# Local attention by probabilities times shifted inputs, with Wv Wo folded per head and the score mask copied into PSUM

## The chip, the cores and the metric

One Trainium2 chip, one of its cores. The metric is the time of one execution on the device in microseconds (us), the median of several executions; lower is better.

## The reference, cut to what matters

Input x is 4 sequences of 512 rows of 128 numbers, float32. A first attention with relative positions (16 heads of 8) comes first; the change doesn't touch it. Then come six layers. Each takes x through a local attention and a feed-forward part and adds both:

```python
half 64 columns of x are shifted down by one row (shift_tokens), then
q, k, v = x @ Wqkv                       # 16 heads of 64
q = l2norm(q) * q_scale; k = l2norm(k) * k_scale; both rotated (rotary, with scales)
sim = q k^T * 8    for windows of 32 queries, against their own 32 and the 32 keys before
sim = masked where key > query or key < query - 32, or no key there
out = softmax(sim) @ v ;  x += out @ Wo
h = layernorm(shifted x) @ W1 + b1 ;  a, gate = split(h)
x += (a * gelu(gate)) @ W2 + b2
```

`softmax(sim) @ (x Wv) @ Wo` per head equals `(softmax(sim) @ x) @ (Wv Wo)`, with x the shifted input; the changed kernel uses the right side.

## The kernel before, in words

The kernel has two parts: the first attention (to about 458 us) and `local_layers`, which holds the six layers. In the layers work is cut into tiles of 128 rows: 16 tiles per layer (4 sequences, called batches or groups, of 4 tiles), 96 tiles in all. Everything is float32. PE turns each float32 product into two records, each with its own weight load; a turn (transposition by the identity) is one.

Each engine runs a list of its own, written out by hand: a loop over rounds n (`for n in PERIODS`), in which each engine does its parts of tiles n+2 to n-4 in a fixed order, and waits on semaphores where it needs another's result. Some work comes once in four rounds, by `step = n % 4`: the feed-forward part of a whole batch (hidden products, gelu, gates, down projection) and its statistics and normalising. PSUM holds three pairs of banks (`ring`, rooms 0 to 2) and two single banks (`tpose`, `yps`). `ROOM` says which result lives in which room; `take` waits until the result that was there before has been read (`FREED`).

What is done for a tile, by engine and line of the profile:

- PE: `turn_x` (L454) turns x; `project` (L463) makes K, V and Q, two products of 512 columns each; `turn_qk` (L473) turns the rotated Q or K, eight 128x128 turns; `scores` first writes the mask as eight bf16 products (L491) and adds 64 small products of queries and keys onto it (L499, 128 records, in two halves); `turn_p` (L510) turns the probabilities; `attend` (L529) makes 64 products of V and turned probabilities (128 records, in two halves); `project_out` (L541) makes eight products with Wo. By the batch: `shift` (L551, L553), `turn_xn` (L561), `hidden` (L569, twelve records of 512 columns), `project_ffn` (L579, 24 records).
- VectorE (DVE): `rotate` (L643) multiplies Q or K with the two rotary tables, two passes over 1024 elements; `sum_squares` (L652); `take_max` (L658), `take_scores` (L666, subtracts), `sum_probs` (L674), `invert` (L681), `divide` (L687), `add_y` (L694), and by the batch `statistics` (L701, L705), `offsets`, `gate` (L721) and `add_ffn` (L730).
- ScalarE (ACT): `square` (L317), copies out of PSUM of x, Q, K, V, probabilities and the weighted sum (L328, L329, L335, L344, L355, L369, L376), `exps` (L363), and by the batch `normalise` (L393), `copy_xn` (L384) and `gelus` (L402). The gelu and the exponential each need a load of their function table.
- GpSimd (POOL): `add` (L240) adds the halves of the rotation, two additions each for Q and K; `norms` (L248 to L265) makes the inverse norms in 14 small steps; `scale` (L275) applies them to Q and to K.
- SP issues the copies: 16 per tile put V, row block by row block, where each window finds its own and the previous rows (`windows`), and the weights of the next layer (`load_layer`).

The order of PE in a round, before:

```python
project("K", n); turn_qk(0, n - 1); turn_x(n + 2)      # step 0: hidden(g - 2, 0..2)
attend(n - 3, 0)                                       # step 3: shift, step 1: project_ffn
turn_qk(1, n - 1); attend(n - 3, 1); project("V", n)
scores(n - 1, 0); project("Q", n + 1); scores(n - 1, 1)
turn_p(n - 2)                                          # step 3: turn_xn(g - 1)
project_out(n - 3)
```

## Time and profile before

| | before |
|---|---|
| three runs | 2148.3, 2149.88, 2151.88 us; median 2149.88 |
| the profiled execution | span 2143.9 us; its own time is not listed beside the runs |
| first attention | to about 458 us |
| PE busy | 2022.6 us, 94% of the span, 35763 matmuls |
| DVE, ACT, POOL busy | 1497.0 (70%), 1286.6 (60%), 1522.5 (71%) |
| mean granted TensorE clock | 0.984 |

The span runs from the first to the last instruction of one profiled execution. Busy shares are averages over stages. A timeline row gives the start, the time taken, the engine, the line, the operation, the tiles written and read, shapes and the count of merged instructions; what stands in brackets is the idle time before it and who ended it. Durations of merged rows reach from the first start to the last end, and pipelined instructions overlap a little, so what a group costs is best read from its start to the start of the next.

### The profile page before, as it was taken

What the parts mean: (1) busy time and instruction counts of PE and PEld (TensorE: products, weight loads), DVE (VectorE), ACT (ScalarE), POOL (GpSimd) and SP (SyncE); (2) the same over time, 40 slices, a digit from 0 to 9 for tenths busy, and PEclk for the clock granted to TensorE, in tenths of its full rate; (3) what the DMA queues carried; (4) which work ended last, traced back from release to release, by engine and by line L of the source; (5) the groups of instructions that cost most, each with busy time, mean ns of one, the idle gap of its engine ahead of it and who ended that gap; (6) DMA issues with size and microseconds to landing.
All of it is one profiled execution on the core that took longest, in us unless ns stands there. A gap on an engine that the chain in (4) does not pass through costs nothing.

```text
span 2143.9 us, 84229 instructions
## 1 busy us (share of the span) xinstructions
PE 2022.6 (94%) x35763; PEld 1356.1 (63%) x35763; DVE 1497.0 (70%) x2268; ACT 1286.6 (60%) x1844; POOL 1522.5 (71%) x2307
## 2 busy tenths in 40 slices
PE   4789999878999999999999999999999999999997
PEld 1455555545666667666766667666676666766675
DVE  2445454458877887777877787777877788778773
ACT  3567777634656665665656565566656666566653
POOL 3344444458878887788877778778887788777880
PEclk8899999998999999999999999999999999999998
DMA  4999999932323222242222422224222242222221
GB/s 125 289 347 355 344 357 344 348 126 61 74 62 111 68 65 65 63 113 67 72 62 62 113 62 69 65 62 120 63 66 62 63 117 70 62 62 63 68 72 43
DMA packets 120004, 261.51 MB, mean 122 GB/s; under 512 B 29092, under 2 KB 34128, under 8 KB 118864
## 3 DMA queue, kind: packets, MB, share of 16 engines
q1 hardware_dynamic: 119632, 256.13, 41.4%
q8 instruction: 285, 4.67, 1.0%
q14 instruction: 87, 0.71, 0.1%
HBM read 87.06 MB, written 68.29 MB: 72 GB/s over the span
## 4 chain that ended last, share of the span: by engine, by line
PE 68%; POOL 4%; DVE 3%; issue 2%; ACT 1%; POOLq 0%; DVEq 0%; ACTq 0%
PE ring L463 22%; PE ring L529 9%; PE ring L473 8%; PE yps L541 7%; PE ring L499 7%; PE ring L569 5%; PE ring L510 4%; PE tpose L579 3%; PE ring L491 1%; POOL roped L275 1%; DVE turned L643 1%; PE tpose L551 1%; DVE ss L652 1%; DVE stats L701 0%; POOL ss L248 0%
## 5 line engine op out<-in xcount | busy, mean ns | idle before, releaser
L643 DVE TENSOR_TENSOR turned<-ring,ropes 128x1024 f32<-128x1024 f32 x384 | 452.0, 1219 | 303.0 <-PE ring L463 303.0
L240 POOL TENSOR_TENSOR roped<-turned 128x512 f32<-128x512 f32 x384 | 522.5, 1386 | 170.4 <-PE ring L473 169.0
L463 PE MATMUL ring<-wqkv,xT 128*128 128x512 f32 x1152 | 567.4, 616 | 5.2 <-ACT xT L328 4.0
L275 POOL TENSOR_TENSOR roped<-roped,rnorm 128x1024 f32<-128x1024 f32 x192 | 361.5, 1904 | 7.5
L1170 POOL TENSOR_SCALAR less<-less,lowest 128x512 f32<-128x512 f32 x256 | 175.3, 697 | 240.0 <-DVE lowest L1139 240.0
L1139 DVE CUSTOM_DVE_ANT_0 less<-ps_b,shifted 128x512 f32<-128x512 f32 x256 | 166.6, 688 | 226.0 <-PE ps_b L1002 79.7
L463 PEld LDWEIGHTS ring<-wqkv,xT 128*128 128x128 f32 x1152 | 198.2, 192 | 161.0 <-issue 149.8
L369 ACT COPY pT<-ring 128x1024 f32<-128x1024 f32 x96 | 97.2, 1012 | 305.8 <-PE ring L510 305.8
L529 PEld LDWEIGHTS ring<-pT,vwin 64*64 64x64 f32 x12288 | 198.5, 134 | 51.9 <-issue 51.5
L317 ACT ACTIVATE squares<-ring 128x1024 f32<-128x1024 f32 x192 | 197.3, 1028 | 55.8 <-DVE turned L643 55.8
L529 PE MATMUL ring<-pT,vwin 64*64 64x32 f32 x12288 | 219.7, 220 | 4.9 <-issue 3.4
L652 DVE TENSOR_REDUCE ss<-squares 128x16 f32<-128x1024 f32 x192 | 221.3, 1184 | 1.2 <-ACT squares L317 0.9
L473 PEld LDWEIGHTS ring<-ident,roped 128*128 128x128 f32 x1536 | 174.5, 142 | 70.0 <-issue 38.4
L473 PE MATMUL ring<-ident,roped 128*128 128x128 f32 x1536 | 204.4, 276 | 8.7 <-ACT qT L335 2.9
L499 PEld LDWEIGHTS ring<-kT,qT 64*32 64x32 f32 x12288 | 139.5, 105 | 100.8 <-issue 99.2
L1002 PE MATMUL ps_b<-posm,qvT 32*128 32x512 f32 x512 | 149.1, 666 | 52.3 <-DVE lowest L1139 43.6
L541 PE MATMUL yps<-wo,oT 128*128 128x128 f32 x1536 | 188.3, 276 | 1.2 <-ACT oT L376 1.1
L541 PEld LDWEIGHTS yps<-wo,oT 128*128 128x128 f32 x1536 | 180.0, 193 | 1.6 <-ACT oT L376 1.6
L499 PE MATMUL ring<-kT,qT 64*32 64x64 f32 x12288 | 173.0, 224 | 4.9 <-issue 4.9
L1068 PEld LDWEIGHTS ps_b<-ident,less 128*128 128x128 f32 x1024 | 111.5, 142 | 94.3 <-POOL less L1170 79.2
L344 ACT COPY kT<-ring 128x1024 f32<-128x1024 f32 x96 | 97.0, 1011 | 100.6 <-PE ring L473 100.6
L1213 ACT ACTIVATE pT_a<-ps_b 128x512 f32<-128x512 f32 x256 | 141.3, 613 | 25.3 <-PE ps_b L1068 25.2
(133 smaller groups left out, 3234.7 us busy)
## 6 DMA issues: line engine op xcount, KB each, us to landing
vwin<-v SPq DMA_DIRECT2D x1536, 64.0 KB, 2.0
shifted<-scratch_w SPq DMA_DIRECT2D x64, 1024.0 KB, 12.6
scratch_w<-wrows SPq DMA_DIRECT2D x48, 1026.0 KB, 10.9
scratch_w<-x SPq DMA_DIRECT2D x16, 1026.0 KB, 10.4
wqkv<-in_l_wqkv SPq DMA_DIRECT2D x6, 1536.0 KB, 6.9
wo<-in_l_wo SPq DMA_DIRECT2D x6, 512.0 KB
w<-in_l_w SPq DMA_DIRECT2D x6, 342.0 KB
w<-in_l_w SPq DMA_DIRECT2D x6, 171.0 KB
```

Of the source, the lines that this page charges most:

```text
L240: nc.gpsimd.tensor_tensor(halves[2][:, :, side, :], halves[0][:, :, side, :], halves[1][:, :, 1 - side, :], ALU.add).then_inc(s[name + "_a ...
L275: nc.gpsimd.tensor_tensor(whole, whole, norm, ALU.mult).then_inc(s[name + "_roped"], 1)
L317: nc.scalar.activation(squares[:, n, :], ring[:, room(name.upper()), :, :].rearrange("p b c -> p (b c)"), ACT.Square).then_inc(s[name + "_ ...
L463: last = nc.tensor.matmul(out[:, half, :], xT[:, t % SEQT * P:(t % SEQT + 1) * P], wqkv[:, layer_of(t), at + half * 512:at + (half + 1) * ...
L473: last = nc.tensor.transpose(out[:, j * P:(j + 1) * P], roped[:, n, j * P:(j + 1) * P], ident[:, :])
L499: last = nc.tensor.matmul(out[W * win:W * win + W, r, j * W2:(j + 1) * W2], qT[rows, j, W * win:W * win + W], kT[rows, j, at:at + W2], sta ...
L529: last = nc.tensor.matmul(out[a * DH:(a + 1) * DH, r, at:at + W], vwin[rows, p, win, j * DH:(j + 1) * DH], pT[rows, j, W * win:W * win + W ...
L541: last = nc.tensor.matmul(out[:, 0:D], oT[:, j % 2, j // 2, :], wo[:, layer_of(t), j, :], start=j == 0, stop=j == PAIRS - 1)
L643: ins = nc.vector.tensor_tensor(turned[:, n, part, :].rearrange("p (h d) -> p h d", d=DH), heads, table, ALU.mult)
L652: nc.vector.tensor_reduce(ss[:, n * HEADS:(n + 1) * HEADS], squares[:, n, :].rearrange("p (h d) -> p h d", d=DH), AX.X, ALU.add).then_inc( ...
L1139: nc.vector.tensor_tensor_reduce(less[:, c % 2, k, :], ps[:, 2 + k, :], shifted[:, c // 2 % NR, k, c % 2, :], -SCALE0, HIGHEST, ALU.add, A ...
L1170: nc.gpsimd.tensor_scalar(less[:, c % 2, k, :], less[:, c % 2, k, :], -1.0, lowest[:, c % 2, k:k + 1], ALU.mult, ALU.add).then_inc(s["scal ...
```

## The change

V is no longer projected. Instead each head's Wv Wo (128x128) is made once per layer: Wv is turned by PE (`turn_wv`), copied by ACT, multiplied with Wo (`make_wvo`) and copied into `wvo`. Five DMA copies per tile (16 before) put the shifted input of the tile, and the same 32 rows earlier, into `xs`. The weighted sum (`attend`) is eight products of 32 rows by 512 columns: for each window of 32 rows, x of the window (stationary) times the probabilities of all 16 heads and 32 queries. The four windows lie in four row groups of PE and write to four banks. ACT copies the result in two pieces (`copy_o` OA, OB), and the output is then sixteen products (`project_out`, in two halves) instead of eight.

The probabilities are turned by VectorE in 32x32 blocks (`turn_p` there), straight into SBUF; PE's turns of them and ACT's copy go away. The mask isn't multiplied in by PE any more: ACT copies it into the scores' banks (`write_masks`), and the products add onto it. The scores' banks are now room 0, which K uses too, so the mask waits until VectorE has rotated the next tile's K.

VectorE's rotation waits for ACT's squaring (before, ACT's squaring waited for the rotation). The rotated Q and K have two buffers (`roped`). The order of all engines' lists is rewritten: Q's rotation moves to the end of VectorE's list, POOL's additions go ahead of the norms and act on tile n instead of n-1, the hidden products move from step 0 to step 1 and the down projection from step 1 to step 2. The bf16 identity and two mask fills of the tables go away. Cut to its core:

```diff
-        ROOM = {"K": 0, "QT": 1, "XT": 4, "H0": 2, "H1": 1, "H2": 0, "O": 2, "XS": 3, "F": 3, "KT": 1, "V": 0, "S": 2, "Q": 1, "PT": 0, "XN": 3, "Y": 4}
-        FREED = {"Q": ("q_squared",), "K": ("k_squared",), "V": ("v_copied",), "QT": ("qT_copied",),
-                 "KT": ("kT_copied",), "S": ("scores_taken",), "PT": ("p_copied",), "O": ("oT_copied",),
+        prev_in = [s[f"prev{n}"] for n in range(NX)]
+        OWN, PREV, LOADS = 3 * 16, 2 * 16, 10 * 16
+        CLEARED = 4
+
+
+        ROOM = {"K": 0, "QT": 1, "XT": 4, "H0": 1, "H1": 2, "H2": 0, "OA": 1, "OB": 2, "XS": 3, "F": 3, "KT": 2, "S": 0, "Q": 1,
+                "XN": 3, "Y": 4, "T": 1, "M0": 1, "M1": 2}
+        FREED = {"Q": ("q_rotated",), "K": ("k_rotated",), "QT": ("qT_copied",),
+                 "KT": ("kT_copied",), "S": ("scores_taken",), "OA": ("oa_copied",), "OB": ("ob_copied",),
                  "H": ("gelu_made", "h_ready"), "XT": ("xT_copied",), "XN": ("xnT_copied",), "XS": ("xn_made",), "Y": ("y_added",),
-                 "F": ("x_done",)}
+                 "F": ("x_done",), "T": ("wvT_copied",), "M": ("wvo_copied",)}
...
+                at_least(sp, s["o_summed"], t - NX + 1)
+                at_least(sp, prev_in[(t - NX + 1) % NX], PREV * ((t - NX + 1) // NX + 1) if t >= NX else 0)
+                sp.dma_start(xs[:, a, 0, 0:half], x[:, here, 0:half]).then_inc(s["own_in"], 16)
+                sp.dma_start(xs[1:P, a, 0, half:D], x[0:P - 1, here, half:D]).then_inc(s["own_in"], 16)
+                first = zero[P - 1:P, :] if t % SEQT == 0 else x[P - 1:P, before, half:D]
+                sp.dma_start(xs[0:1, a, 0, half:D], first).then_inc(s["own_in"], 16)
+                sp.wait_ge(s["own_in"], OWN * (t + 1))
+                sp.dma_start(xs[W:P, a, 1, :], xs[0:P - W, a, 0, :]).then_inc(prev_in[a], 16)
+                sp.dma_start(xs[0:W, a, 1, :], xs[P - W:P, b, 0, :]).then_inc(prev_in[a], 16)
...
-                    at_least(pool, s[name + "_turned"], t)
+                    at_least(pool, s[name + "_turned"], t - 1)
...
-                norms(n - 2)
-                scale(0, n - 2)
-                scale(1, n - 2)
+                add(0, n)
+                add(1, n)
+                norms(n)
+                scale(0, n)
+                scale(1, n)
+                if step == 3:
+                    deviations(g - 1)
                 if step == 1:
                     add_b2(g - 2)
-                add(0, n - 1)
-                add(1, n - 1)
-                if step == 0:
-                    deviations(g - 2)
...
-                    act.wait_ge(s[name + "_rotated"], t + 1)
+                    act.wait_ge(s[name + "_made"], t + 1)
...
+            def write_masks(t):
+
+                if live(t):
+                    n = t + 1
+                    if live(n):
+                        act.wait_ge(s["k_rotated"], n + 1)
+                    at_least(act, s["scores_taken"], t)
+                    if n % SEQT == 1 and lives(n // SEQT - 2):
+                        act.wait_ge(s["h_ready"], FCH * (n // SEQT - 1))
+                    rows = bias[:, 1 if t % SEQT == 0 else 0, :, :].unsqueeze(1).broadcast_to([P, 2, PAIRS, W2])
+                    nc.scalar.copy(ring[:, room("S"), :, :].rearrange("p r (j k) -> p r j k", k=W2), rows).then_inc(s["masked"], 1)
+
+            def copy_o(kind, t):
+
                 if live(t):
                     act.wait_ge(s["o_summed"], t + 1)
                     at_least(act, s["y_made"], t)
-                    nc.scalar.copy(oT[:, :, :, :].rearrange("p r m c -> p (r m c)"),
-                                   ring[:, room("O"), :, :].rearrange("p b c -> p (b c)")).then_inc(s["oT_copied"], 1)
+                    at = W2 if kind == "OB" else 0
+                    nc.scalar.copy(oT[:, :, at:at + W2].rearrange("c h (b q) -> c b h q", q=W),
+                                   ring[:, room(kind), :, :].rearrange("c b (h q) -> c b h q", q=W)
+                                   ).then_inc(s["oa_copied" if kind == "OA" else "ob_copied"], 1)
...
-                if step == 0:
-                    normalise(g - 2)
-                copy_p(n - 3)
-                if step == 0:
+                copy_x(n + 2)
+                square(1, n)
+                if step == 1:
                     copy_xn(g - 2)
-                square(0, n)
-                exps(n - 2)
                 copy_q(n - 1)
-                square(1, n)
-                if step == 0:
+                copy_k(n - 1)
+                copy_wv(product_layer(n, 2))
+                copy_wvo(product_layer(n, 1))
+                if step == 1:
                     gelus(g - 2, 0)
                     gelus(g - 2, 1)
                     gelus(g - 2, 2)
-                copy_k(n - 1)
-                copy_o(n - 3)
-                copy_x(n + 2)
-                copy_v(n)
+                write_masks(n - 1)
+                copy_o("OA", n - 2)
+                copy_o("OB", n - 2)
+                square(0, n + 1)
+                exps(n - 1)
+                if step == 0:
+                    normalise(g - 2)
...
+            def turn_wv(layer):
+
+                if layer is not None:
+                    pe.wait_ge(s["weights"], LOADS * (layer + 1))
+                    out = take("T", layer).rearrange("p b c -> p (b c)")
+                    for j in range(PAIRS):
+                        last = nc.tensor.transpose(out[:, j * P:(j + 1) * P], wv[:, j * P:(j + 1) * P], ident[:, :])
+                    last.then_inc(s["wv_turned"], 1)
+
+            def make_wvo(layer):
+
+                if layer is not None:
+                    pe.wait_ge(s["wvT_copied"], layer + 1)
+                    for half in range(2):
+                        out = take("M", layer, half)
+                        for j in range(half * PAIRS // 2, (half + 1) * PAIRS // 2):
                             for r in range(2):
-                                at = DH * r + W * (win % 2)
-                                first = t % SEQT == 0 and win == 0
-                                nc.tensor.matmul(out[W * win:W * win + W, r, :], identb[at:at + W, at:at + W],
-                                                 bias[at:at + W, 1 if first else 0, :, :].rearrange("p h k -> p (h k)"),
-                                                 start=True, stop=False, skip_group_check=True)
-                    for j in range(half * PAIRS // 2, (half + 1) * PAIRS // 2):
+                                rows, at = slice(r * DH, (r + 1) * DH), j % (PAIRS // 2) * D
+                                last = nc.tensor.matmul(out[:, r, at:at + D], wvT[rows, j, :], wo[rows, j, :], start=True, stop=True)
+                        last.then_inc(s["wvo_made"], 1)
...
+            def scores(t):
+                if live(t):
+                    pe.wait_ge(s["qT_copied"], t + 1)
+                    pe.wait_ge(s["kT_copied"], t + 1)
+                    pe.wait_ge(s["masked"], t + 1)
+                    out = take("S", t)
...
+            def attend(t):
+
+                if live(t):
+                    pe.wait_ge(s["p_turned"], t + 1)
+                    pe.wait_ge(prev_in[t % NX], PREV * (t // NX + 1))
+                    outs = (take("OA", t), take("OB", t))
+                    for own in (1, 0):
+                        for win in range(WT):
+                            rows = slice(W * win, W * win + W)
+                            last = nc.tensor.matmul(outs[win // 2][:, win % 2, :], xs[rows, t % NX, 1 - own, :],
+                                                    pT[rows, own, :, :].rearrange("p h q -> p (h q)"),
+                                                    start=own == 1, stop=own == 0, skip_group_check=True)
+                    last.then_inc(s["o_summed"], 1)
+
+            def project_out(t, half):
+
+                if live(t):
+                    if half == 0:
+                        pe.wait_ge(s["oa_copied"], t + 1)
+                        pe.wait_ge(s["ob_copied"], t + 1)
+                        pe.wait_ge(s["wvo_copied"], 2 * (t // (SEQT * BATCH) + 1))
+                        take("Y", t)
+                    out = view("Y")
+                    for h in range(half * PAIRS, (half + 1) * PAIRS):
+                        r, j = h // PAIRS, h % PAIRS
+                        last = nc.tensor.matmul(out[:, 0:D], oT[:, h, :], wvo[:, layer_of(t), r, j, :],
+                                                start=h == 0, stop=h == HEADS - 1)
...
+                turn_x(n + 2)
                 project("K", n)
+                if step == 1:
+                    turn_xn(g - 2)
+                project_out(n - 3, 0)
                 turn_qk(0, n - 1)
-                turn_x(n + 2)
-                if step == 0:
+                turn_qk(1, n - 1)
+                turn_wv(product_layer(n, 2))
+                make_wvo(product_layer(n, 1))
+                if step == 1:
                     hidden(g - 2, 0)
                     hidden(g - 2, 1)
                     hidden(g - 2, 2)
-                attend(n - 3, 0)
+                if step == 2:
+                    project_ffn(g - 2)
                 if step == 3:
                     shift(g - 1)
-                if step == 1:
-                    project_ffn(g - 2)
-                turn_qk(1, n - 1)
-                attend(n - 3, 1)
-                project("V", n)
-                scores(n - 1, 0)
+                project_out(n - 3, 1)
+                attend(n - 2)
+                scores(n - 1)
                 project("Q", n + 1)
-                scores(n - 1, 1)
-                turn_p(n - 2)
-                if step == 3:
-                    turn_xn(g - 1)
-                project_out(n - 3)
...
-                    dve.wait_ge(s[name + "_made"], t + 1)
+                    dve.wait_ge(s[name + "_squared"], t + 1)
...
+            def turn_p(t):
+
+                if live(t):
+                    dve.wait_ge(s["p_normed"], t + 1)
+                    at_least(dve, s["o_summed"], t)
+                    nc.vector.transpose(pT[:, :, :, :], probs[:, t % 2, :, :].rearrange("p h (o k) -> p o h k", k=W)
+                                        ).then_inc(s["p_turned"], 1)
...
+                    if (t + 1) % SEQT:
+                        dve.wait_ge(s["own_in"], OWN * (t + 2))
...
-                if step == 2:
-                    add_ffn(g - 2)
-                rotate(0, n)
-                take_max(n - 2)
-                take_scores(n - 2)
-                add_y(n - 4)
+                sum_probs(n - 2)
+                invert(n - 2)
+                divide(n - 2)
+                turn_p(n - 2)
+                sum_squares(0, n)
                 rotate(1, n)
+                sum_squares(1, n)
+                if step == 0:
+                    offsets(g - 2)
+                add_y(n - 3)
                 if step == 3:
                     statistics(g - 1)
-                sum_probs(n - 2)
-                invert(n - 2)
-                sum_squares(0, n)
-                if step == 0:
+                if step == 1:
                     gate(g - 2, 0)
                     gate(g - 2, 1)
                     gate(g - 2, 2)
-                sum_squares(1, n)
-                if step == 3:
-                    offsets(g - 1)
-                divide(n - 2)
+                if step == 2:
+                    add_ffn(g - 2)
+                take_max(n - 1)
+                take_scores(n - 1)
+                rotate(0, n + 1)
```

## Rows read from the trace of the kernel before

**Rows 1.** The page, part 4: shares of the chain of waits, by engine.
```profile
PE 68%; POOL 4%; DVE 3%; issue 2%; ACT 1%; POOLq 0%; DVEq 0%; ACTq 0%
```

**Rows 2.** Timeline of PE: K projections four tiles apart (start us, us, engine, line).
```profile
590.65 1.88 PE L463 MATMUL ring<-wqkv,xT 128*128 128x512 f32 x4
...
658.91 1.88 PE L463 MATMUL ring<-wqkv,xT 128*128 128x512 f32 x4
```

**Rows 3.** Timeline of PE, one tile, and the hidden products of another.
```profile
1252.32 0.41 PE L491 MATMUL ring<-bias,identb 32*32 32x512 bf16 x8
...
1253.57 1.98 PE L463 MATMUL ring<-wqkv,xT 128*128 128x512 f32 x4
1255.49 0.86 PE L499 MATMUL ring<-kT,qT 64*32 64x64 f32 x64
1256.27 1.09 PE L510 MATMUL ring<-ident,probs 128*128 128x128 f32 x8
1257.20 1.95 PE L541 MATMUL yps<-wo,oT 128*128 128x128 f32 x16
1258.99 1.88 PE L463 MATMUL ring<-wqkv,xT 128*128 128x512 f32 x4
...
1261.78 1.14 PE L529 MATMUL ring<-pT,vwin 64*64 64x32 f32 x64
...
1277.60 5.31 PE L569 MATMUL ring<-xnT,w 128*114 128x512 f32 x12
```

**Rows 4.** Timeline of PE, first attention: first of eight records, and what follows.
```profile
107.61 0.69 PE L1002 MATMUL ps_b<-posm,qvT 32*128 32x512 f32 x1
...
108.68 0.55 PE L1068 MATMUL ps_b<-ident,less 128*128 128x128 f32 x3
```

**Rows 5.** Timeline of VectorE, one tile.
```profile
1257.87 1.21 DVE L658 TENSOR_REDUCE smax<-ring 128x16 f32<-128x1024 f32 x1
1259.11 1.22 DVE L666 TENSOR_TENSOR probs<-ring,smax 128x1024 f32<-128x1024 f32 x1
...
1260.91 2.35 DVE L643 TENSOR_TENSOR turned<-ring,ropes 128x1024 f32<-128x1024 f32 x2 [0.38 <-PE ring L463]
...
1265.42 1.17 DVE L674 TENSOR_REDUCE rsum<-probs 128x16 f32<-128x1024 f32 x1
...
1266.79 2.28 DVE L652 TENSOR_REDUCE ss<-squares 128x16 f32<-128x1024 f32 x2
...
1269.05 1.22 DVE L687 TENSOR_TENSOR probs<-probs,rinv 128x1024 f32<-128x1024 f32 x1
```

**Rows 6.** Groups by form, 800 to 1900 us; last, ACT's busy time in one normalising.
```profile
L363 ACT ACTIVATE probs<-probs 128x1024 f32<-128x1024 f32 x64 | 67.8, 1059 | 38.3 <-DVE probs L666 38.1
...
L721 DVE SCALAR_TENSOR_TENSOR hT<-ring,b,gelu 114x512 f32<-114x512 f32 x51 | 36.7, 747 | 13.5 <-ACT gelu L402 13.5
...
L402 ACT ACT_TABLE_LOAD x17 | 21.8, 1283 | 0.3
...
1269.00:1272.60 3.60, 2.60 (x8) 1.00 0.37 90
```

**Rows 7.** Timeline, an addition of POOL and the division that began in it.
```profile
1285.21 1.27 POOL L240 TENSOR_TENSOR roped<-turned 128x512 f32<-128x512 f32 x1 [3.18 <-PE ring L473]
1285.46 2.11 DVE L687 TENSOR_TENSOR probs<-probs,rinv 128x1024 f32<-128x1024 f32 x1
```

**Rows 8.** Timeline of POOL: first step of the norms, and the two scalings.
```profile
1253.21 0.22 POOL L253 TENSOR_SCALAR rnorm<-ss 128x32 int32<-128x32 int32 x1
...
1257.39 3.76 POOL L275 TENSOR_TENSOR roped<-roped,rnorm 128x1024 f32<-128x1024 f32 x2
```

**Rows 9.** Windows: length, busy us (x instructions) of each engine, PEclk, DMA share, GB/s.
```profile
1214.00:1216.40 2.40, 0.43 (x28) 0.32 (x20) 1.88 (x1) 0.43 (x1) 2.40 (x2) 1.00 0.28 98
...
1217.40:1218.40 1.00, 1.00 (x2) 0.36 (x2) 0.00 (x0) 0.84 (x3) 1.00 (x2) 0.54 0.27 66
...
110.00:113.00 3.00, 0.00 (x0) 0.00 (x0) 1.31 (x4) 0.89 (x2) 0.60 (x1) 1.00 1.07 329
```

208 lines of the change are left out of this document (81 added, 127 removed).

## The prediction

> **What bounds the kernel now.** I read the page's chain first: TensorE (PE) holds 68% of the chain that ended last, VectorE (DVE) 3%, GpSimd (POOL) 4% [rows 1]. Matmul records are modelled and say little of how full PE is, so next came PE's timeline in the layers. Four tiles, among them one with the hidden products of a batch and one with its down projection, take 68.3 us from one K projection to the fourth after it [rows 2]. Inside a tile there is no hole of note: each group begins where the one before ends [rows 3]. PE's own work sets the pace; the timelines of the other engines show pauses, PE's does not. Less the hidden products, 5.3 [rows 3], the down projection (24 records, 2.7 at the pace of the output's 16 in 1.79) and some 1.4 of small turns, a plain tile is 14.7.
>
> **What the change takes from PE.** Per tile: the V projection 1.92 (same form as Q, which has 1253.57 to 1255.49), the mask products 0.34, the eight probability turns 0.93 (L510 to L541), two halves of the weighted sum at 1.14 [rows 3]: 5.5 us. It adds eight more pairs of output products, 1.79 (L541 to the next K) [rows 3], and the new weighted sum: 16 records of 32 rows by 512 columns in four row groups. Eight such records of the first attention took 1.07 us, four at a time [rows 4], so 2.15. The other bound is one after the other at Q's pace (four records in 1.92): 7.7. I take 2.15, because rows 4 show the overlap itself, in this shape. PE's work falls by 1.5 per tile, to some 62.3 per four.
>
> **What takes PE's place.** The order closes a ring over four engines, because K of tile n+1 and the scores of tile n now share a pair of banks. ScalarE (ACT) may write the mask there only when VectorE has rotated that K. VectorE rotates K late in its list, behind the tile-before's whole softmax, its new 32x32 turn and a sum of squares. The scores wait for the mask, and VectorE's list begins with the maximum over them. Once round, from the last score product (time 0) to the next:
>
> - Maximum to 1.25, subtraction to 2.5 [rows 5].
> - PE has projected Q by 1.9 [rows 3]; ACT squares it, 1.06 like its other 128x1024 pass [rows 6], to 3.0. The rotation now waits for the squaring: VectorE loses 0.5. Q's rotation 2.35, to 5.3; sum and inversion 1.37, to 6.8; division 1.22, to 8.0 [rows 5].
> - The turn is in no row. VectorE's passes over 1024 elements take 1.2, Q's double pass 2.35 [rows 5]; it could be nothing at best and the double pass at worst. I take 1.25, the single pass being nearest: 9.3.
> - Sum of squares 1.14, to 10.4; K's rotation 2.35, to 12.8 [rows 5].
> - The mask on ACT: 1.06 as its other pass [rows 6], since only operands differ; bounds nothing and twice that. To 13.9. Scores, 2 x 0.8 (1255.49 to 1256.27) [rows 3], to 15.5.
>
> Behind the waiting mask in ACT's list stand the two copies of the weighted sum, the next Q's squaring and the exponential. The copies (2.1) run beside scores and Q projection, so the wait for the mask costs nothing beyond itself.
>
> **A block inside the ring.** The division that began 0.25 us after an addition of POOL took 2.11 instead of 1.22: about the rest of that addition, then its own time [rows 7]. In the new order POOL is in its second scaling when the division is due: it adds K's halves (2 x 1.27 [rows 7]) once K is rotated, 2.8 before the round begins, then the norms (4.2 and a clamp), then two scalings, 3.76 together [rows 8], and ends at 7.9. The division asks at 6.8: 1.1 lost, a ring of 16.5. The bounds are no block, 15.5, and a whole scaling, 17.4; I take what the positions give. The Trainium skill, SBUF — State Buffer, section SBUF: two separate sides, says that whoever comes first keeps the pair of ports shared by VectorE and GpSimd for its whole instruction; by that rule the wait may last a whole scaling, where the trace shows it only against an addition, and a round would be up to 17.4. The Trainium skill, Vector Engine (DVE) Microarchitecture Reference, section 3.8, has the 32x32 turn stream one element per cycle per lane; an estimate from it and 0.96 GHz is 1.07 us for 1024 elements, and a round would be 0.2 shorter than by my 1.25.
>
> **The four rounds of a batch.**
> - *To step 0*: nothing else, 16.5.
> - *To step 1*: ACT ends the exponential at 3.9, normalises 2.6 [rows 6], copies the next x in two small pieces (an estimate, 0.5), 7.0. Only then can the first output half start, for its bank is x's: 8.8. Turns of Q and K 2 x 0.9, 10.5; Q's copy out 10.9; hidden products 5.31 [rows 3], 16.3; second output half, 18.1. VectorE's addition of y waits for that half and stands ahead of the gates: 0.3, gate 0.75, the third gelu 0.7 (it needs a buffer back), gate 0.75 [rows 6], 20.7. Only then may the mask be written (it takes the third hidden bank): 21.8; scores 23.5.
> - *To step 2*: a table load, 1.28 [rows 6], ahead of the exponential, 5.2; x copies 5.7; output half 7.5; turns 9.3; down products 12.0; output half 13.8; weighted sum 16.0; scores 17.7. PE sets this round.
> - *To step 3*: after two long rounds POOL is ahead, its scaling ends at 6.9, the block goes: 15.5, with the statistics 15.6.
>
> Sum 73.3 against 68.3: 5.0 more per batch, +120 for 24 batches. The step-1 round carries it: PE's hidden products and both output halves stand in one file with ACT's normalising and VectorE's gates, which the order before kept beside each other.
>
> **Edits by the layer.** Eight turns of Wv and 32 half-height records per layer, 3 us of PE, with ACT's copies in banks that the turned Q and K must leave first: 1.3 in the PE-bound round (0.9 and a wait for Q's copy), 1.2 in the next. 2.5 x 5 layers: +12. In the first layer they stand ahead of the first projection and behind all weight loads: +6. Bounds 0 and 40 for both. Costed at nothing: SP issues 5 copies per tile for 16, and they begin two rounds (over 30 us) ahead of use; were that cover gone, a round would wait for two copies in a row. VectorE's addition of y also waits for one of them, three rounds old by then. POOL's earlier additions and the second roped buffer lie in POOL's slack of 2 to 3 us per round, between Q's and K's additions.
>
> **The sum.** Span 2143.9 + 120 + 12 + 6 = 2282 for this execution. The median of the runs shown, 2149.9, is 6.0 above its span (no other time of that execution is shown): 2288, rounded 2290.
>
> **Rivals.**
> - *PE still sets the pace* (the other side, faster). Then time follows PE's work: 24 x 6.0 less, 18 back, 2149.9 - 126 = 2024. For it: PE's 68% of the chain. Against: VectorE's list with mask and scores, laid end to end from rows 3, 5 and 6, is 15.5 against a plain tile's 14.7 now. It decides at a ring under 14.7 and a step-1 round under 20. 0.09.
> - *The clock falls.* PE would idle some 2 us before each plain round's scores, and for x in step 1. A hole of 2 us was followed by a granted clock of 0.54, mostly its 1.2 GHz level; another of 3 us kept 1.00 [rows 9]. A fall adds some 1.5 to Q's projection, on the ring, and 1.7 to the step-1 file. In most batches: 1.5 to 3 per batch, 2325 to 2360. 0.25.
> - *The row groups don't overlap*: 5.5 more per weighted sum, which passes the mask in every round, about 3.5 each on average: +14 per batch, 2625. Rows 4 speak against. 0.02.
> - *Gain and ring cancel* (the step-1 round near 18.5): 2150, within 0.2%. 0.03.
>
> **How the numbers follow.** My ring with its blocks has 0.61 and its own range of 2235 to 2335; without any block it is 1.2 less per batch, 2260. The range 2215 to 2365 adds the clock's case at the top, and at the bottom two rounds of a batch a microsecond shorter without block. Outside lie the faster rival and the serial sum. Faster by over 0.2% (about what a measurement of this kernel can tell from no change) 0.10, within 0.03, slower 0.87.
>
> **What would show it.** In the profile after: VectorE's share of the chain far over 3%, with ACT's mask in it; four K projections some 73 us apart, one round of 22 to 24 among them; PE waiting at the scores for ACT, ACT's mask waiting for the rotation, VectorE's rotation of Q waiting for the squaring; divisions with a mean near 2. I am wrong if PE stays without holes, if the mask does not wait for the rotation, or if the step-1 round is under 19; and partly wrong if the clock falls each round.

## The result, and the profile after

The changed kernel takes 2388.98 us (median of 4 runs, 2381.33 to 2401.34) against 2149.09 for the one before on the same chip (2143.15 to 2151.88): 1.112 times as long, 95% interval 1.109 to 1.116. The sign was forecast, the size not: 240 us more instead of 140, and 24 over the top of the range. The first attention, which neither the change nor any edit touches, ended between 450 and 476 us in the traces of all versions, so ten us between two versions can come from there.

The page of the changed kernel, its busy times, the granted clock by slices and the chain; then, from part 5, groups with their mean in ns and the idle time ahead of them:

```profile
PE 1946.2 (81%) x24867; PEld 1305.6 (55%) x24867; DVE 1688.2 (71%) x2364; ACT 1287.4 (54%) x1860; POOL 1489.8 (62%) x2306
...
PEclk7899999979999999999999999999999999999998
...
PE 40%; DVE 19%; ACT 12%; issue 7%; POOL 1%; DMA 0%; SPq 0%; DVEq 0%; ACTq 0%; POOLq 0%
...
L542 PE MATMUL ring<-kT,qT 64*32 64x64 f32 x12288 | 153.9, 230 | 107.8 <-ACT ring L384 84.8
...
L384 ACT CAST ring<-bias 128x1024 f32<-128x1024 bf16 x96 | 97.6, 1017 | 252.1 <-DVE turned L675 232.4
...
L716 DVE TENSOR_TENSOR probs<-probs,rinv 128x1024 f32<-128x1024 f32 x96 | 190.3, 1983 | 3.3
```

TensorE (PE) fell from 94% to 81% of a longer span and from 68% to 40% of the chain [rows 1]; VectorE (DVE) rose from 3% to 19%, ScalarE (ACT) from 1% to 12%. The scores wait for the mask and the mask for VectorE's rotation of K: the ring is there. The mean granted clock is 0.954, before 0.984.

The same from PE's side, the waits in total (us, times, longest):

```profile
PE ring L542 <- ACT ring L384: 84.8, 47, 2.6
PE tpose L593 <- ACT xn L425: 62.0, 24, 6.2
PE ring L497 <- DVE probs L697: 57.0, 75, 0.9
...
PE ring L556 <- ACT gelu L434: 41.2, 23, 1.8
...
PE ring L542 <- issue: 20.7, 12, 2.8
```

Now two rounds. First VectorE's timeline from one maximum to the next, the round that ends in step 0:

```profile
1544.59 1.22 DVE L690 TENSOR_REDUCE smax<-ring 128x16 f32<-128x1024 f32 x1 [0.19 <-PE ring L542]
...
1547.41 2.35 DVE L675 TENSOR_TENSOR turned<-ring,ropes 128x1024 f32<-128x1024 f32 x2 [0.34 <-ACT squares L339]
...
1551.21 2.33 DVE L716 TENSOR_TENSOR probs<-probs,rinv 128x1024 f32<-128x1024 f32 x1
1553.57 1.25 DVE L724 STREAM_TRANSPOSE pT<-probs 128x1024 f32<-128x1024 f32 x1
1554.74 1.18 DVE L684 TENSOR_REDUCE ss<-squares 128x16 f32<-128x1024 f32 x1
1555.84 2.34 DVE L675 TENSOR_TENSOR turned<-ring,ropes 128x1024 f32<-128x1024 f32 x2
...
1560.99 1.22 DVE L690 TENSOR_REDUCE smax<-ring 128x16 f32<-128x1024 f32 x1 [1.26 <-PE ring L542]
```

K's rotation ends at 1558.2, the mask is copied from 1558.22 to 1559.24, the scores run to 1560.9. Every term is within 0.2 of the forecast's: 16.4 us for the round.

Then PE's timeline of the round that follows, to step 1, the one with the hidden products:

```profile
1555.32 2.00 PE L556 MATMUL ring<-pT,xs 32*128 32x512 f32 x16
1559.49 1.47 PE L542 MATMUL ring<-kT,qT 64*32 64x64 f32 x128 [2.17 <-ACT ring L384]
1560.89 1.98 PE L497 MATMUL ring<-wqk,xT 128*128 128x512 f32 x4
...
1563.62 1.96 PE L497 MATMUL ring<-wqk,xT 128*128 128x512 f32 x4 [0.64 <-DVE probs L697]
1567.51 0.63 PE L593 MATMUL tpose<-ident,xn 128*128 128x128 f32 x4 [1.94 <-ACT xn L425]
1567.98 3.57 PE L572 MATMUL yps<-wvo,oT 128*128 128x128 f32 x16
1571.34 2.01 PE L507 MATMUL ring<-ident,roped 128*128 128x128 f32 x16
1573.67 5.38 PE L602 MATMUL ring<-xnT,w 128*114 128x512 f32 x12 [0.32 <-ACT qT L356]
1578.88 1.95 PE L572 MATMUL yps<-wvo,oT 128*128 128x128 f32 x16
1582.62 2.00 PE L556 MATMUL ring<-pT,xs 32*128 32x512 f32 x16 [1.79 <-ACT gelu L434]
1584.72 1.59 PE L542 MATMUL ring<-kT,qT 64*32 64x64 f32 x128
```

Of the two output halves (L572) the first took 3.57 us from its first start to its last end (3.36 to the start of what follows), the second 1.95: the same 16 records. Windows over the hole ahead of the first and over the half itself (length, busy us of each engine, granted clock, DMA share, GB/s):

```profile
1565.57:1567.51 1.94, 0.01 (x1) 0.03 (x1) 1.91 (x3) 1.94 (x7) 1.94 (x2) 1.00 0.00 0
...
1567.98:1571.34 3.36, 3.36 (x19) 3.36 (x17) 3.33 (x2) 1.54 (x2) 3.36 (x3) 0.52 0.01 2
```

PE had idled 1.94 us, the granted clock in the half was 0.52, its level of 1.2 GHz. Of the 22 such rounds between 600 and 2340 us, 12 had the slow half. In 8 of the other 10 the Q projection at the round's start, behind the 2.2 us in which PE waits for the mask, took 3.3 to 3.8 instead of 1.98. Two had neither, and those two rounds took 23.9 and 24.3 where the others took 25.2 or more: half clock costs 20 of 22 batches some 1.6 us.

How the rounds of most versions stand: the medians of 21 rounds of each kind (tiles 7 to 91; the columns go by tile, for the kernel before too), each from the start of one maximum on VectorE to the next, and the time for the first eight tiles.

```
                       to step 1  step 2  step 3  step 0   sum   tiles 0-8
before                    17.3     14.5    15.2    20.4    67.5    126.9
forecast                  23.5     17.7    15.6    16.5    73.3
after                     25.6     17.6    15.5    16.5    75.2    158.5
K rotated first           23.8     17.6    15.5    14.7    71.6    144.5
K twice                   25.1     17.6    15.6    16.7    75.0    160.1
short output half         24.1     16.6    16.5    17.0    74.2    155.5
mask alone, on before     17.4     14.8    15.5    20.7    68.3    126.1
three orders              20.5     17.8    15.5    14.7    68.5    144.4
first norms in holes      25.5     17.6    15.6    16.6    75.3    145.6
holes filled              23.9     17.7    15.6    16.6    73.8    156.0
mask by TensorE           24.1     18.1    16.1    16.1    74.4    155.4
outputs ahead of K        20.4     15.7    16.2    14.5    66.8    145.0
orders, mask by TensorE   20.8     16.2    16.3    14.4    67.7    135.0
all edits                 20.3     15.8    15.6    14.4    66.0    127.0
```

### The profile page after: what moved, and what is told of

It reads as the page before. It is cut to its first block, busy times and chain, and to the rows that moved or that the text cites. A ratio compares the mean times of both kernels' runs of the same rounds, so it can differ in the third digit from the quotient of the medians.

```text
span 2388.4 us, 61609 instructions
## 1 busy us (share of the span) xinstructions
PE 1946.2 (81%) x24867; PEld 1305.6 (55%) x24867; DVE 1688.2 (71%) x2364; ACT 1287.4 (54%) x1860; POOL 1489.8 (62%) x2306
## 4 chain that ended last, share of the span: by engine, by line
PE 40%; DVE 19%; ACT 12%; issue 7%; POOL 1%; DMA 0%; SPq 0%; DVEq 0%; ACTq 0%; POOLq 0%
PE ring L497 9%; DVE turned L675 9%; PE yps L572 9%; PE ring L542 6%; PE ring L602 6%; PE ring L556 4%; DVE probs L716 3%; ACT squares L339 3%; PE ring L507 3%; PE tpose L612 3%; ACT xn L425 3%; DVE rsum L705 2%; ACT ring L384 2%; DVE ss L684 2%; ACT qT L356 1%
## 5 line engine op out<-in xcount | busy, mean ns | idle before, releaser
L497 PE MATMUL ring<-wqk,xT 128*128 128x512 f32 x768 | 407.3, 656 | 61.7 <-DVE probs L697 57.0
L572 PEld LDWEIGHTS yps<-wvo,oT 128*128 128x128 f32 x3072 | 380.6, 200 | 88.6 <-issue 84.7
L572 PE MATMUL yps<-wvo,oT 128*128 128x128 f32 x3072 | 396.7, 285 | 30.1 <-ACT xT L350 27.7
L497 PEld LDWEIGHTS ring<-wqk,xT 128*128 128x128 f32 x768 | 141.3, 205 | 225.5 <-issue 216.4
L690 DVE TENSOR_REDUCE smax<-ring 128x16 f32<-128x1024 f32 x96 | 117.5, 1224 | 191.8 <-PE ring L542 189.0
L542 PE MATMUL ring<-kT,qT 64*32 64x64 f32 x12288 | 153.9, 230 | 107.8 <-ACT ring L384 84.8
L384 ACT CAST ring<-bias 128x1024 f32<-128x1024 bf16 x96 | 97.6, 1017 | 252.1 <-DVE turned L675 232.4
L556 PE MATMUL ring<-pT,xs 32*128 32x512 f32 x1536 | 192.5, 615 | 48.9 <-ACT gelu L434 41.2
L392 ACT COPY oT<-ring 128x1024 f32<-128x1024 f32 x192 | 184.7, 1013 | 48.7 <-PE ring L556 48.7
L356 ACT COPY qT<-ring 128x1024 f32<-128x1024 f32 x96 | 97.3, 1014 | 190.1 <-PE ring L507 190.0
L716 DVE TENSOR_TENSOR probs<-probs,rinv 128x1024 f32<-128x1024 f32 x96 | 190.3, 1983 | 3.3
```

The costliest lines, as they stand in the source:

```text
L392: nc.scalar.copy(oT[:, :, at:at + W2].rearrange("c h (b q) -> c b h q", q=W), ring[:, room(kind), :, :].rearrange("c b (h q) -> c b h q", q=W)
L497: last = nc.tensor.matmul(out[:, half, :], xT[:, t % SEQT * P:(t % SEQT + 1) * P], wqk[:, layer_of(t), at + half * 512:at + (half + 1) * 5 ...
L542: last = nc.tensor.matmul(out[W * win:W * win + W, r, j * W2:(j + 1) * W2], qT[rows, j, W * win:W * win + W], kT[rows, j, at:at + W2], sta ...
L556: last = nc.tensor.matmul(outs[win // 2][:, win % 2, :], xs[rows, t % NX, 1 - own, :], pT[rows, own, :, :].rearrange("p h q -> p (h q)"), ...
L572: last = nc.tensor.matmul(out[:, 0:D], oT[:, h, :], wvo[:, layer_of(t), r, j, :], start=h == 0, stop=h == HEADS - 1)
L716: nc.vector.tensor_tensor(whole, whole, rinv[:, :].unsqueeze(2).broadcast_to([P, HEADS, W2]), ALU.mult).then_inc(s["p_normed"], 1)
```

## The experiments

My theory after the result: the ring and PE's file set the rounds as forecast, and the rest is half clock behind PE's holes. The rivals: PE's work is what counts after all; or the order of the step-1 round was mispriced in itself.

The runs were made on several chips, on which the kernel before took 2144 to 2149 us. Ratios are against it on the same chip. Differences in us are taken between the medians as measured; by the ratios those from the changed kernel are up to 7 us smaller.

**Is it the ring? K rotated ahead of the sum of Q's squares.**

```diff
                 turn_p(n - 2)
-                sum_squares(0, n)
                 rotate(1, n)
+                sum_squares(0, n)
                 sum_squares(1, n)
```

> Only VectorE's list differs: the sum of Q's squares stands behind K's rotation instead of ahead of it; no work is added or taken. Theory (the ring VectorE, ACT's mask, PE's scores sets the rounds leading to step 0 and step 3): the mask comes 1.1 us earlier, those two rounds go from 16.4 and 15.5 to about 15.3 and 14.5, the rounds to step 1 and step 2 (set by a file of PE and ACT) stay at 25.5 and 17.6. Two rounds of 1.1 in 24 batches: 2389 - 53 = 2336. Rival (PE's doubled output products and its waits for weights set the time, whatever the mask does): no change, 2389.

Measured 2288.56 us, ratio 1.067 (1.065 to 1.070): 100 less, by exchanging two instructions on one engine that neither add nor remove work. The ring is shown for the round to step 0. That round lost 1.9, more than the 1.14 moved: the division's block fell from 2.21 to 2.00 as well, and Q's rotation no longer waited for its squaring (0.41 before). The round to step 3, for which 14.5 was expected, stayed at 15.5. There the scores ended earlier, but the maximum began no sooner, because VectorE came to it without any idle time (0.19 in the changed kernel): VectorE's own list, with the statistics of the batch, sets that round. The round to step 1 lost 1.8, of which the output half explains most: the hole ahead of the scores shrank, and 3 of 22 output halves were slow instead of 12, with no slow projection ahead of the others. Of the 104 us between the two traces 76 lie in tiles 8 to 92, 14 in the first eight tiles and 13 ahead of the first maximum, 12 of these in the first attention. So some 12 of the 100 may not be the exchange's.

**Second output half ahead of the hidden products.**

```diff
                 if step == 1:
+                    project_out(n - 3, 1)
                     hidden(g - 2, 0)
...
-                project_out(n - 3, 1)
+                if step != 1:
+                    project_out(n - 3, 1)
                 attend(n - 2)
```

> Only PE's list differs, and only at step 1: the second output half stands ahead of the hidden products. Theory (in the step-1 round the gates stand behind VectorE's addition of y, which waits for that half): the gates run beside the hidden products, the round goes from 25.5 to about 24.0, others stay: 2389 - 36 = 2353. Rival (PE's amount of work sets that round): the same products in another order, no change, 2389.

Measured 2356.02, ratio 1.099 (1.096 to 1.101). The round to step 1 went from 25.6 to 24.0, the others stayed.

**K projected twice in the hole of the step-1 round.** The same result is written twice.

```diff
-                project("K", n)
+                project("K", n, 2 if step == 1 else 1)
```

> At step 1 K is projected twice over into the same banks, 1.8 us of PE work more per batch, in the hole in which PE now waits for the normalised x. Clock theory (the hole of 1.9 us is followed by the 1.2 GHz level, at which the first output half takes 3.4 instead of 1.8): the hole is gone, the half is back at 1.8, the round goes from 25.5 to about 23.9: 2389 - 38 = 2351, though PE does more. Rival (the output half is slow for another reason, its weights or its bank): the round stays at 25.5 or grows by up to 1.8, 2389 to 2432.

Measured 2366.29, ratio 1.103 (1.102 to 1.105): PE does 1.8 us more per batch and the kernel is 23 us faster, against the rival. But not the 38 of the theory. The timeline of PE shows where some of the rest went:

```profile
1544.37 1.67 PE L542 MATMUL ring<-kT,qT 64*32 64x64 f32 x128 [2.16 <-ACT ring L384]
1545.97 3.40 PE L497 MATMUL ring<-wqk,xT 128*128 128x512 f32 x4
...
1554.48 1.99 PE L572 MATMUL yps<-wvo,oT 128*128 128x128 f32 x16
```

The output half is back at 1.99 in all 22 rounds, and the Q projection behind the other hole is slow in 14 of them (11 in the changed kernel). Of the eight rounds without a slow one, seven took 23.7 to 24.3 and one, with a hole in the scores, 25.9; the others took 24.7 or more.

**Normalising a round later.** ScalarE's `normalise` moves from the end of step 0's list to behind the copy of x in step 1's, the copy of Q goes ahead of `copy_xn`, and in PE's list `turn_xn` goes behind the first output half and the turn of Q.

```diff
                 copy_x(n + 2)
+                if step == 1:
+                    normalise(g - 2)
                 square(1, n)
...
                 exps(n - 1)
-                if step == 0:
-                    normalise(g - 2)
```

> ACT normalises behind the copies of the next x instead of ahead of them, and PE turns the normalised x behind the first output half and the turn of Q. No work is added or taken. Theory (in the step-1 round the whole file waits 2.6 us for the normalising, and the hole lowers the clock): the output half starts 2.6 us earlier and at full clock; the hidden products then wait for the normalised, turned and copied x at about 9.8, and start about 1.5 us or more earlier than the 12.7 of now: the round goes from 25.5 to 22 to 23.5: 2389 - 48 to - 84, 2305 to 2341. Rival (PE's amount of work): no change.

Measured 2347.9, ratio 1.096 (1.093 to 1.098), 41 less, where 48 to 84 were expected. No output half was slow any more (0 of 22), but 19 of 177 Q and K projections were (over 2.5 us; 18 of 178 in the changed kernel).

**PE's work alone: seven products of the second output half left out.**

```diff
-                    for h in range(half * PAIRS, (half + 1) * PAIRS):
+                    for h in range(half * PAIRS, half * PAIRS + (PAIRS if half == 0 else 1)):
```

> The changed kernel with 7 of the 8 products of the second output half left out (the output lacks them): 1.57 us less of TensorE's work per tile, nothing else. My theory (the ring VectorE, ScalarE, TensorE sets the rounds to step 0 and to step 3, TensorE's file those to step 1 and to step 2): the rounds of 16.5 and 15.5 stay, those of 25.5 and 17.6 lose 1.6 each, 3.1 per batch, 24 batches, 2389 - 75 = 2314. Rival (TensorE's load sets every round): 1.57 in all four, 2389 - 151 = 2238. Second rival: nothing moves because the longer hole lets the clock fall in more rounds, 2370 to 2390.

Measured 2354.11, ratio 1.099 (1.097 to 1.100). The theory that PE's load sets the rounds asked for 151 us less and got 35: it falls. But neither did the ring's 75 come. The rounds to step 1 and 2 lost 1.4 and 1.0; those to step 3 and 0 grew by 0.9 and 0.5. The growth to step 3 is the division's block come back: with the rounds before it shorter, GpSimd's (POOL's) first scaling began at 4.1 after the maximum instead of 2.9 (tile 50), and the division took 2.19 instead of 1.23 (medians). To step 0 it was the clock: PE's hole ahead of the scores before it was 2.6 instead of 1.1, and the Q projection behind them was slow in 10 of 21 rounds instead of 3. Windows of this kernel, over the hole ahead of the scores and over the Q projection behind them:

```profile
1523.60:1526.20 2.60, 0.06 (x4) 0.00 (x0) 2.60 (x4) 1.19 (x2) 1.15 (x1) 1.00 0.08 17
1527.73:1531.20 3.47, 3.47 (x8) 1.45 (x6) 2.51 (x3) 0.15 (x1) 2.57 (x12) 0.53 0.10 24
```

28 of 179 Q and K projections took over 2.5 us, 18 of 178 in the changed kernel; the mean clock was 0.937.

**The products Wv Wo of layer 0 alone.**

```diff
-            return layer if at == 0 and 0 <= layer < DEPTH else None
+            return layer if at == 0 and layer == 0 else None
```

> The changed kernel with Wv Wo computed in layer 0 alone and used in all six (the values of the other layers are wrong): the eight turns, 32 products and three copies at each of 5 layer boundaries are left out. My prediction had 2.4 us for each boundary, 12 in all: 2377. Rival: the irregular rounds at the boundaries (holes with a slow clock behind them) hang on these pieces, up to 28 more: 2349.

Measured 2377.28 (2363.4 to 2384.1), ratio 1.108 (1.104 to 1.112): 12 less by the medians and 7 by the ratios, and the intervals of the two kernels overlap, so the term of 12 is neither refuted nor clearly confirmed. The rival's further 28 didn't come.

**The mask part alone, on the kernel before.** ScalarE copies the mask, PE's mask products are gone. The output isn't the reference's in this version, and why wasn't looked into; instructions and sizes are those of the change, so the time alone is read.

```diff
                 copy_o(n - 3)
+                write_masks(n - 1)
                 copy_x(n + 2)
```

> The kernel before with only the mask part of the change: ScalarE copies the mask into the scores' banks, TensorE's mask products are gone, banks and order as they were. Theory A (TensorE sets the pace before, ScalarE's copy is ready in time): 0.34 us less per tile, 96 tiles, 2145 - 33 = 2112. Theory B (the copy, 1.02 us, waits for the scores' banks and stands ahead of the scores): some 0.5 us more per tile, 2190 or over; then the mask's place in ScalarE's list costs wherever the banks are freed late, not only with the changed kernel's ring.

Measured 2178.24, ratio 1.017 (1.015 to 1.019): slower by 34, where 33 faster would have been PE's account. The waits name it:

```profile
PE ring L501 <- ACT ring L386: 51.3, 93, 2.4
```

In 93 of 96 tiles PE waits 0.55 us for the copy, which is more than the 0.34 that it is spared. That makes 51 less 33, 18 of the 34 us; the rest isn't explained. So at this place in ScalarE's list the part costs without the ring too.

**Three orders together** (K rotated first, output half first, normalising later).

> The changed kernel with the three reorderings of the earlier runs together: K rotated ahead of the sum of Q's squares (it gave 100), the second output half ahead of the hidden products (33), normalising a round later (41). If they act in different places: 2389 - 174 = 2215. If the second and the third shorten the same file (the end of the step-1 round through VectorE's addition of y and the gates), only the larger of the two counts: 2389 - 141 = 2248. Both over the 2149 of the kernel before, whose four rounds sum to 67.5; this one would have 69 to 70.5.

Measured 2224.94, ratio 1.038 (1.035 to 1.041): 164 less of the 174 that they gave singly. The medians sum to 68.5, 1.0 over the kernel before.

**Q rotated before it is squared**, on top of these. ScalarE's list has the exponential first, Q's squaring behind it, and both ahead of the next round's copy of x:

```diff
-                square(0, n + 1)
                 exps(n - 1)
+                square(0, n + 1)
```

> The three orders together (2225) and besides Q rotated by VectorE before ScalarE squares it, the exponential ahead of that squaring. The rotation then waits for the projection alone: 0.5 us off the ring. If the ring sets all four rounds: 2225 - 24 x 2.0 = 2177. If the rounds to step 1 and to step 2 hang on TensorE's file, only two gain: 2201. Rival: Q's turn now waits for the squaring (its bank), which ends a microsecond later than before: no gain, 2225.

Measured 2303.08, ratio 1.073 (1.071 to 1.076): 78 slower than without. VectorE's wait went away as meant, but ScalarE now waits for the rotation, and x's copy, behind it in the list, came 1.8 us late for PE in nearly every round:

```profile
PE yps L572 <- ACT xT L350: 162.9, 91, 2.2
```

None of my alternatives had this: I had looked at whom the squaring frees and not at what is queued behind it.

**Both output halves ahead of K, x turned and copied behind the scores**, on the three orders.

```diff
-                turn_x(n + 2)
-                project("K", n)
-                project_out(n - 3, 0)
+                project_out(n - 3, 0)
+                project_out(n - 3, 1)
+                project("K", n)
...
                 scores(n - 1)
+                turn_x(n + 2)
```

> The three orders together (2225) and both output halves ahead of K's projection, the next x turned and copied behind the scores. They fill the 0.6 to 0.9 us in which K waits for the scores' bank, and wait for ScalarE's copy of x no more (1.1 to 1.3 in the round to step 2, as many to step 1 there): the rounds to step 1 and to step 2 lose 1 to 1.5 each, the other two 0: 2225 - 24 x 2 to 3 = 2153 to 2177, with fewer holes ahead of ScalarE's work and perhaps less half clock. Rival: x's copies (0.5) now stand ahead of Q's squaring on the ring and every round gains that: +0.3 x 4 x 24, 2200 to 2250.

Measured 2192.38, ratio 1.021 (1.018 to 1.025), between the two forecasts. The round to step 2 lost 2.1; that to step 3 grew by 0.7, and the division in it took 2.02 instead of 1.36. VectorE now waits ahead of the maximum only in the round to step 1 (3.1); in the others the median wait is 0.1 or nothing. So VectorE's own list, with the waits inside it, sets three rounds of four here, and the scores are ready when it comes to them.

**Both of these edits.**

> Both of the foregoing together. If they add: 2225 - 96 = 2130, under the 2145 of the kernel before; this is the version that could beat both. If K's later projection (it ends at 7.4 after the last score product instead of at 4.3) puts its squaring and rotation on the ring, 2177 or more.

Measured 2188.23, ratio 1.019 (1.016 to 1.021), not to be told from the foregoing. With x's copy out of the way the other edit does no harm, and no good by itself.

**The first normalisings in VectorE's holes**, on the changed kernel.

```diff
+                if 1 <= n < BATCH:
+                    first_norm(n)
                 take_max(n - 1)
                 take_scores(n - 1)
                 rotate(0, n + 1)
-                if 1 <= n < BATCH:
-                    first_norm(n)
```

> The changed kernel with VectorE's normalising of the inputs of batches 1 to 3 (3.8, 3.0 and 4.2 us, once each in the first three rounds) moved from behind Q's rotation to ahead of the maximum, where VectorE idled 5.5, 4.8 and 1.9. I had costed the first rounds at the plain ring. Theory (they stand on the ring): 8.7 less, the first eight tiles 150 instead of 158.5, 2380. Rival (the slow clock and TensorE's waits set these rounds): no change in the eight tiles, 2389.

Measured 2372.13, ratio 1.105 (1.102 to 1.107): 17 less, the first eight tiles 145.6 instead of 158.5. Three groups of four small instructions stood on the ring; the order before had hidden them.

**Both holes filled.** K twice in step 1, and the weighted sum made twice in step 0.

```diff
-                attend(n - 2)
+                attend(n - 2, 2 if step == 0 else 1)
```

> The changed kernel with K projected twice in the round to step 1 and, new, the weighted sum made twice in the round to step 0, where TensorE then waited 2.2 us for the mask: TensorE does 3.8 us more per batch, the result is the same, nothing waits for more. Theory (half clock after holes costs time): K doubled alone gave 23 us back, but moved half of the slow stretch to the Q projection behind the other hole (3.4 instead of 1.98); with both holes filled neither runs slowly: 1.6 per batch from the output half and the irregular rounds besides, 2330 to 2350, granted clock over 0.97. Rival (only the sum of work counts, or the doubled products are late): 2366 or more.

Measured 2366.66, ratio 1.101 (1.099 to 1.103). The rounds say what the theory said, PE's timeline of the step-1 round first:

```profile
1541.43 1.98 PE L497 MATMUL ring<-wqk,xT 128*128 128x512 f32 x4
...
1544.27 3.67 PE L497 MATMUL ring<-wqk,xT 128*128 128x512 f32 x8 [0.74 <-DVE probs L697]
1548.06 0.63 PE L593 MATMUL tpose<-ident,xn 128*128 128x128 f32 x4
1548.53 2.00 PE L572 MATMUL yps<-wvo,oT 128*128 128x128 f32 x16
```

None of the 22 output halves was slow, 5 single projections were, the mean clock was 0.977, and the round to step 1 took 23.9: 1.65 less, and 0.4 over the forecast's 23.5. In 15 of the 22 rounds to step 1 it was 23.7 to 24.0. So the 1.6 us of half clock are shown. The total missed the 2330 to 2350: 1.6 in 24 batches would be 38, and 22 came. Of the rest some 6 are in the rounds to the other steps, which were 0.06 to 0.13 longer each, 4 lie behind tile 92's maximum, and 5 in holes inside the scores that nothing in the profile releases. The round to step 1 was 25.9 to 26.5 in each of the last four batches, with such a hole:

```profile
2172.64 1.51 PE L542 MATMUL ring<-kT,qT 64*32 64x64 f32 x122
2176.05 0.31 PE L542 MATMUL ring<-kT,qT 64*32 64x64 f32 x6 [1.90 <-issue]
```

**The mask by TensorE again**, in the changed kernel: ScalarE's copy out, the eight mask products back at the head of the scores.

```diff
-                write_masks(n - 1)
...
-                    pe.wait_ge(s["masked"], t + 1)
                     out = take("S", t)
+                    for win in range(WT):
+                        for r in range(2):
+                            at = DH * r + W * (win % 2)
+                            first = t % SEQT == 0 and win == 0
+                            nc.tensor.matmul(out[W * win:W * win + W, r, :], identb[at:at + W, at:at + W],
+                                             bias[at:at + W, 1 if first else 0, :, :].rearrange("p h k -> p (h k)"),
+                                             start=True, stop=False, skip_group_check=True)
```

> The changed kernel with the mask part undone: TensorE's eight mask products (0.34 by the kernel before) start the scores, ScalarE's copy (1.02) is gone. They too wait for K's rotation, so the ring is 0.68 shorter: rounds 15.9 to step 0, 14.9 to step 3, 24.9 to step 1; to step 2, where TensorE set the pace, 0.3 longer. 24 x 1.7 = 41 less: 2348. Rival A (the shorter holes keep the clock up, as in the first experiment, which gave twice its ring share): 2300 to 2330. Rival B (the mask copy was no part of what the rounds wait for): no change, 2389.

Measured 2353.32, ratio 1.095 (1.094 to 1.097): 36 less, near the 41, but by other rounds than I had. To step 1 it was 1.4 shorter (2 slow output halves of 22, no slow projection), to step 0 only 0.4, to step 3 0.6 longer. In the round to step 3 VectorE has no idle time ahead of the maximum, and its division took 1.95 instead of 1.23: the block again. In the round to step 0 GpSimd is next: K's turn waits for its scaling.

```profile
1608.33 1.09 PE L506 MATMUL ring<-ident,roped 128*128 128x128 f32 x8
1611.17 1.09 PE L506 MATMUL ring<-ident,roped 128*128 128x128 f32 x8 [1.75 <-POOL roped L297]
```

**Toward a better version.** First the outputs ahead of K, the first normalisings in the holes and the mask by TensorE, then Q rotated first besides.

> The version with both output halves ahead of K (2192) with VectorE's first normalisings in its holes (they gave 13) and the mask by TensorE. In it the mask stood on the ring in the rounds to step 1 and to step 3 and in that to step 0 little: 0.7 x 2 to 3 x 24 = 34 to 50. 2192 - 13 - 34 to 50 = 2129 to 2145, level with the kernel before or under it. Rival: TensorE's work and the holes in its instruction stream set these rounds by now, 2175.

Measured 2182.95, ratio 1.016 (1.014 to 1.018): above my range, 8 over the rival's 2175. The regular rounds sum to 67.7, 0.8 more than with the outputs ahead of K alone (66.8); the first normalisings act only ahead of tile 8. So in this order the mask by TensorE gave nothing to the regular rounds.

> The foregoing with Q rotated before it is squared as well. That gave 4 us with the outputs ahead of K: 2125 to 2141. Rival: 2171 or more, since K's squaring and copy stand behind Q's squaring on ScalarE, and the rounds to step 1 were 0.5 longer with it.

Measured 2155.32 (12 runs, 2149.02 to 2165.85), ratio 1.0041 (1.0022 to 1.006): better than I had expected against the foregoing, but 0.4% slower than the kernel before, and the fastest with the new form of the attention. Its layers are ahead of it: from tile 8 to tile 92 it took 1413.7 us where the kernel before took 1428.5 (changed kernel 1613.2). It gives that back behind: from the last maximum to the end 52.4 us, 42.1 before. In PE's timeline the hidden products of the batch before (2103.0 to 2110.7) stand between the last scores and the last weighted sum. Reordering those last rounds wasn't tried. Why the Q edit gave 28 us here and 4 there isn't settled. The traces show one difference: with the edit the division of the round to step 1 took 1.23 here (2.18 without it) and 2.81 there (2.15 without it).

## Why the prediction was wrong, and where it was right

- **What bounds.** Right that PE bounds before and no longer does after: the exchange of two VectorE instructions (100 us) and the 7 left-out products (35 of 151) show it from both sides. The ring through mask and scores sets the round to step 0. In that to step 3 VectorE waited only 0.19 ahead of the maximum: its own list was nearly as long as the ring, so a shorter ring gave nothing there. The forecast didn't have that.
- **PE's terms.** The weighted sum, 2.15 by the first attention's rows [rows 4], took 2.00 for 16 records: the row groups overlap. Output halves 1.8, mask copy 1.02 for 1.06.
- **The ring.** Right in each term: Q's rotation waited 0.26 to 0.41 for its squaring (medians of the rounds to step 2, 3 and 0; forecast 0.5), the turn took 1.25, of which 1.17 to the start of the next (1.25), the blocked division 2.33 (2.3). Rounds to step 0, 3 and 2 came to 16.5, 15.5 and 17.6 where 16.5, 15.6 and 17.7 stood.
- **The division's block.** In all but one of the 96 divisions of the changed kernel the wait was at most 1.2 us, against scalings of 1.9 each, and their mean was 1.98 where an unblocked one takes 1.22 [rows 5]: the rest of an instruction under way, as I had it from the addition [rows 7]. In the version with both edits of Q and outputs some took up to 2.91, a wait of 1.7 and nearly a whole scaling. The port rule of the Trainium skill (SBUF — State Buffer, SBUF: two separate sides) lets VectorE wait for the end of GpSimd's whole instruction; by that rule, the trace agrees, though the round of 17.4 that it would allow was no regular one here. The stream turn, which I had estimated at 1.07 from the Trainium skill (Vector Engine (DVE) Microarchitecture Reference, section 3.8), was measured at 1.17 from start to start.
- **The round to step 1: the step that failed.** I had 23.5, it took 25.55 (median). Its file is as I laid it out up to the first output half, at 7.0 after the maximum as forecast. That half was priced at full clock, 1.8, and took 3.36. With both holes filled the round is 23.9. So 1.65 is the clock, shown by that run. The other 0.4 is the order, by the timeline alone: the weighted sum also waits for the second gate, whose bank it takes, and ends 0.2 after the mask. I had forgotten that wait. 2.05 x 24 = 49 of the 106 us by which the span was missed.
- **The clock was a rival and should have been in the sum.** I gave it 0.25 and prices of 1.5 and 1.7 per fall, which hold; the sum itself had nothing for it. Its own range, 2325 to 2360, was passed by 29 as well, since the clock is only 38 of the 106. What I got wrong was how often: I had two holes of 2 to 3 us with opposite outcome [rows 9] and left it out of the sum. In the changed kernel there are two such holes 6 us apart in each batch, and one of the two was followed by half clock in 20 of 22.
- **The irregular rounds.** A regular batch takes 75.2, the mean over tiles 7 to 91 is 76.9. PE's holes inside the scores with no releaser were 11 with 18.4 us in all in the layers, 5 with 4.9 before. Behind six of the eight of over 1.5 us the Q projection was slow too. I had nothing for them.
- **The first tiles.** Priced as plain rounds; the first eight took 31.6 more than before, where two batches' 10 and the first layer's 6 stood. The first normalisings are 13 of the rest.
- **The tail.** From tile 92's maximum to the end 107.8 instead of 88.0, where 5 stood. The last step-1 rounds have no other work beside them. Seen in the timeline, not tested.
- **The layer's products.** +12; the run without them gave 12 by the medians and 7 by the ratios, and doesn't decide.
- **The mask.** I priced it only inside the ring. On its own it makes the kernel before slower by 34 us, and without it the changed kernel is 36 faster. With the outputs ahead of K it does no harm: there the mask by TensorE made the regular rounds 0.8 longer per batch.

The miss of 106 by the trace: 43 in the step-1 rounds of tiles 8 to 92 and some 24 in irregular rounds there, half clock and holes in the scores among them; 16 in the first eight tiles, 13 of them the first normalisings; 15 at the end; and 8 ahead of the first maximum, 4.5 of them because the first attention, which the change doesn't touch, ended later.

## What to carry to other kernels

When a change shortens the busiest engine's work and closes a ring through others, it also opens holes in that engine, and on TensorE a hole of 2 us can be paid for twice: once itself, and once by what runs at half clock behind it (1.6 us per batch here). Put that second price into the sum when the trace of before shows it even once. Once the ring is loosened, look at the engine in it with the longest list: VectorE came to have no idle time in three rounds of four. Before moving a step, read what stands behind it in each in-order list: the exchange of two instructions gave 100 us here, and another, with the same reasoning, cost 78.

## What the runs showed of the hardware that I had not expected

- More work made it faster: 1.8 us more of projections per batch, 23 us less in all.
- Filling one of two holes doesn't cure the other: with the first filled the projection behind the second was slow in 14 of 22 rounds (11 before). A shorter PE program (mean clock 0.937) got 35 us of the 75 expected, part of the rest lost to the clock and part to the division's block.
- The holes inside the scores of up to 2.8 us, put down to "issue", are in 128 short records in a row. They were 11 in the changed kernel's layers (600 to 2340 us), 11 in the one with three orders (22 more of 0.2 to 0.4 us there stand at the head of the scores), 6 with the mask products back.
- These holes go with the loading of instructions. In the changed kernel a 16 KB packet of DMA queue q8, of the kind "instruction", began 0.1 to 0.9 us ahead of 8 of the 9 holes of over 0.5 us, where one such packet comes in 11 us; in all kept traces one began between 2 us ahead and 0.6 us behind the start of 150 of 155 such holes. Many packets pass without a hole, and which engine's instructions they bring isn't shown, so the cause is likely and not proven. With a window over one hole the DMA view shows it:

```profile
DMA packets 140, 0.04 MB, mean 14 GB/s; under 512 B 139, under 2 KB 139, under 8 KB 139
...
q8 instruction: 1, 0.02, 2.9%
```

The window is 851.0 to 854.2 us of the changed kernel; the hole is 2.82 us long and ends at 854.1.
